# Reordering the work around the first expert tiles of a gated alignment and mixture-of-experts block on one Trainium2 core

## The reference

```python
x = x + jnp.tanh(g_xattn[0]) * align(ctx_1024, layernorm(x))   # dynamic time warping of 154 rows onto 2048, 2 batches
xn = layernorm(x).reshape(4096, 512)
logits = xn @ gate_w.T                                          # 8 experts
w, sel = jax.lax.top_k(logits, 2); w = softmax(w)
expert_out = jnp.einsum('nc,edc->ned', xn, expert_w)
x = x + jnp.tanh(g_ffn[0]) * (w_full of the two chosen experts summed over expert_out)
```

## Time and profile before

| what | value |
| --- | --- |
| median of 3 runs | 602.07 us (599.56 to 602.33) |
| the profiled execution | 599.65 us, of it 597.9 us span |
| PE busy | 457.6 us, 77% |
| DVE busy | 307.6 us, 51% |
| ACT busy | 263.0 us, 44% |
| POOL busy | 225.5 us, 38% |
| granted PE clock, mean | 0.86 of full |

### The profile page before, as it was taken

How to read it: one execution, slowest core, us unless ns; L and a number is a source line. 1 busy time by engine, 2 the same in 40 slices (tenths; PEclk the granted TensorE clock), 3 DMA queues, 4 the chain that set the end, 5 groups by cost and what they waited for, 6 DMA issues and landing times. The chain is left out here.

```text
span 597.9 us, 8208 instructions
## 1 busy us (share of the span) xinstructions
PE 457.6 (77%) x2029; PEld 271.4 (45%) x2029; DVE 307.6 (51%) x1635; ACT 263.0 (44%) x508; POOL 225.5 (38%) x214
## 2 busy tenths in 40 slices
PE   8989655477232304687996989999999999999980
PEld 7989543254122201343443544444454444445440
DVE  7778799999998885898678411101111010111000
ACT  6538778854735402892653223322233332223320
POOL 5550222000000000003428565766657665767522
PEclk9999868668565655796997999999999999999995
DMA  8965334640046001777999686878868787878743
GB/s 289 353 189 190 86 85 117 187 98 2 0 160 263 1 1 36 288 245 231 296 260 309 116 164 122 149 134 144 138 114 153 130 142 136 139 122 152 118 53 35
DMA packets 61386, 88.88 MB, mean 149 GB/s; under 512 B 24933, under 2 KB 25189, under 8 KB 61181
## 3 DMA queue, kind: packets, MB, share of 16 engines
q0 software_dynamic: 16048, 37.31, 35.8%
q1 hardware_dynamic: 38701, 42.64, 21.8%
q10 hardware_dynamic: 6592, 8.42, 4.5%
HBM read 48.92 MB, written 39.43 MB: 148 GB/s over the span
## 5 line engine op out<-in xcount | busy, mean ns | idle before, releaser
L1973 PE MATMUL psum<-big,work 128*128 x560 | 257.1, 602 | 4.3 <-ACT work L1627 4.3
L697 POOL DMA_INDIRECT stage<-x_rows,row_ids x71 | 70.0, 986 | 224.1 <-DVE row_ids L1173 176.0
L1973 PEld LDWEIGHTS psum<-big,work 128*128 128x128 f32 x560 | 102.9, 194 | 108.0 <-issue 108.0
L1323 DVE TENSOR_TENSOR part_scale<-stage,st 128x1 f32<-128x1 f32 x62 | 10.0, 162 | 201.2 <-DMA stage<-x_rows,row_ids 201.2
L717 POOL DMA_INDIRECT out_dram<-prow,row_ids x34 | 61.3, 1802 | 36.0 <-ACT prow L1638 14.2
L717 POOL DMA_INDIRECT out_dram<-tokens,row_ids x36 | 57.2, 1589 | 41.3 <-DMA out_dram<-tokens 15.5
L1638 ACT ACTIVATE tokens<-psum,tile_shares 128x512 f32<-128x512 f32 x36 | 24.7, 687 | 98.4 <-issue 70.5
L1638 ACT ACTIVATE prow<-psum,tile_shares 128x512 f32<-128x512 f32 x34 | 23.3, 687 | 86.8 <-issue 78.6
L1947 PEld LDWEIGHTS psum<-ident,stage 128*128 128x128 f32 x284 | 35.6, 143 | 40.6 <-issue 33.7
L1756 PE MATMUL psum<-ident,stage 128*128 128x128 f32 x128 | 27.7, 401 | 33.3 <-ACT big L1526 20.5
L1627 ACT COPY work<-psum 128x512 f32<-128x512 f32 x71 | 41.0, 578 | 19.2 <-PE psum L1947 14.8
(11 more groups left out here) (388 smaller groups left out, 649.7 us busy)
## 6 DMA issues: line engine op xcount, KB each, us to landing
tokens<-in_x_dram SPq DMA_DIRECT2D x16, 1024.0 KB, 11.8
stage<-in_L_ffn_expert_w_dram ACTq DMA_DIRECT2D x8, 1024.0 KB, 5.6
out_dram<-tokens SPq DMA_DIRECT2D x8, 1024.0 KB, 9.1
x_rows<-tokens SPq DMA_DIRECT2D x7, 1024.0 KB, 7.3
tokens<-dist_rows SPq DMA_DIRECT2D x52, 64.0 KB, 2.1
dist_rows<-work SPq DMA_DIRECT2D x16, 160.0 KB, 2.0
dist_rows<-prow SPq DMA_DIRECT2D x5, 256.0 KB, 10.5
stage<-x_rows,row_ids POOLq DMA_INDIRECT x71
```

Of the source, the lines that this page charges most:

```text
L697: pool.indirect_dma_start(out=xin[:, n % UX, :], out_offset=None, in_=x1_d[0:T, :] if n < FA else x1_d[:, :], in_offset=bass.IndirectOffse ...
L1973: ins = nc.tensor.matmul(psum[:, UP + n % UP, :], xinT[:, n % UX, c, :], expT[:, bass.ds(own, 1), c, :].rearrange("p o d -> p (o d)"), sta ...
```

## The change

Five orders are changed; no matmul is added or removed.

- PE: `invert_first_shares()` stands behind tile 1's expert, not ahead of it. The alignments of tiles 24 to 31 and `rank()` stand behind tile 2, not tile 3.
- ACT: the squares of tiles 16 to 19 stand ahead of the copy of tile 2; three copies out stand ahead of the ten last squares; two one-element activations load the tables of Sqrt and Exp where they stand; the store of the second batch's pairs of shares stands behind `copy_in(5)`.
- DVE: `first_shares()` stands inside `place_choices`, `scales(1)` between the two `lay_lanes`, `pairs_of(1)` ahead of the sets, `ids()` ahead of `own_tiles()`.
- The sets are laid in halves, each member half followed by its number half, and `invert()` waits for the second half in its middle.
- `ids()` keeps its intermediate in `slotf`, not in `owner`, and no longer waits for `s_own`.

```diff
--- before.py
+++ after.py
@@ -442,8 +442,8 @@
         EARLY = 4
         RING = (4, 5, 0, 1, 2, 3)
         AR = len(RING)
-        SQUARED = [[], [16, 17], [18, 19], [20, 21, 22, 23], [24, 25, 26, 27, 28, 29, 30, 31]]
-        ALIGNED = [[], [22, 23], [], [24, 25, 26, 27, 28, 29, 30, 31]]
+        EARLY_SQUARES, MORE_SQUARES, LATE_SQUARES = range(TB, TB + 4), range(TB + 4, TB + 6), range(TB + 6, NT)
+        ALIGNED = [[], [22, 23], [24, 25, 26, 27, 28, 29, 30, 31]]
         LATE = (4, 5, 2, 3, 4, 5, 4, 5, 6, 4, 5, 6, 4, 5, 6, 4)
         BEFORE = [None if t < 4 else [u for u in range(t) if LATE[u] == LATE[t]][-1:] for t in range(TB)]
         FIRST_IDS = 2 * P
@@ -1210,6 +1210,7 @@
                 lnk(v.tensor_tensor_scan(upto, keep[:, :], total, 0.0, ALU.mult, ALU.add))
                 v.tensor_tensor(place, upto, total, ALU.subtract).then_inc(s_gt, 1)
                 ln[0] += 1
+                first_shares()
                 counts = more.rearrange("p (e m) -> p e m", e=E)
                 lnk(v.tensor_tensor(counts, spread(upto[:, KB - 1:KB], [[KB, E], [0, NT]]),
                                     spread(full[:, 0:1], [[0, E], [1, NT]]), ALU.is_gt))
@@ -1267,19 +1268,18 @@
                     v.tensor_tensor(lanes[h][:, :, q * TB:(q + 1) * TB], pattern,
                                     spread(partf[:, 1, (2 * h + q) * TB:(2 * h + q) * TB + 1], [[0, P], [1, TB]]), ALU.is_equal)
 
-            def lay_members():
-
-                for g in (2, 3):
-                    v.wait_ge(s_out[g], 16)
-                    v.wait_ge(s_rows[g], 16 * (GT if g == GB - 1 else 1))
-                v.wait_ge(s_sq, TB)
-                lnk(v.tensor_tensor(sets[:, :, 0, :], spread(partf[:, 0, 0:1], [[1, KB], [0, JB]]),
-                                    spread(tiles[:, 0:1], [[0, KB], [1, JB]]), ALU.is_equal))
-
-            def lay_numbers():
-
-                v.tensor_tensor(sets[:, :, 1, :], sets[:, :, 0, :], spread(numbers[:, 0:1], [[1, KB], [0, JB]]),
-                                ALU.mult).then_inc(s_numl, 1)
+            def lay_sets(h):
+
+                if h == 0:
+                    for g in (2, 3):
+                        v.wait_ge(s_out[g], 16)
+                        v.wait_ge(s_rows[g], 16 * (GT if g == GB - 1 else 1))
+                    v.wait_ge(s_sq, TB)
+                n, i0 = KB // 2, h * KB // 2
+                lnk(v.tensor_tensor(sets[:, i0:i0 + n, 0, :], spread(partf[:, 0, i0:i0 + 1], [[1, n], [0, JB]]),
+                                    spread(tiles[:, 0:1], [[0, n], [1, JB]]), ALU.is_equal))
+                v.tensor_tensor(sets[:, i0:i0 + n, 1, :], sets[:, i0:i0 + n, 0, :],
+                                spread(numbers[:, i0:i0 + 1], [[1, n], [0, JB]]), ALU.mult).then_inc(s_numl, 1)
 
             def pad_places():
 
@@ -1304,8 +1304,7 @@
 
                 v.wait_ge(s_inv, 2)
                 codes_ = psum[:, 7, JB:2 * JB]
-                later = owner
-                v.wait_ge(s_own, 2)
+                later = slotf[:, 0:JB]
                 lnk(v.tensor_scalar(later, codes_, 0.0, float(B * T), ALU.is_lt, ALU.mult))
                 lnk(v.tensor_tensor(later, later, codes_, ALU.add))
                 ins = v.tensor_copy(rows_ids[:, FA:NSEQ], later)
@@ -1353,20 +1352,19 @@
             lay_first_shares()
             for t in (20, 21):
                 add_context(t)
-            first_shares()
             place_choices()
             for t in range(22, NT):
                 add_context(t)
             pad_places()
             lay_lanes(0)
+            scales(1)
             lay_lanes(1)
-            scales(1)
-            lay_members()
             pairs_of(1)
-            lay_numbers()
+            lay_sets(0)
+            lay_sets(1)
             pads()
+            ids()
             own_tiles()
-            ids()
             mark_tiles()
             for n in range(FA, NSEQ):
                 tile_share(n)
@@ -1642,20 +1640,32 @@
                     nc.scalar.mul(yout(n)[:, HC:C], psum[:, 4, HC:C], scale[:, n:n + 1]).then_inc(s_ye, 1)
 
             copy_in(0)
-            for n in range(NSEQ):
-                if n + 1 < NSEQ:
+            copy_in(1)
+            for t in EARLY_SQUARES:
+                squares(t)
+            copy_in(2)
+            nc.scalar.activation(gates[:, 0:1], eps[:, :], ACT.Sqrt)
+            for t in MORE_SQUARES:
+                squares(t)
+            copy_out(0)
+            copy_out(1)
+            copy_in(3)
+            copy_out(2)
+            for t in LATE_SQUARES:
+                squares(t)
+            root(1)
+            copy_in(4)
+            nc.scalar.activation(gates[:, 0:1], eps[:, :], ACT.Exp)
+            shares(1)
+            copy_out(3)
+            copy_in(5)
+            act.wait_ge(s_pair, 2)
+            act.dma_start(x1_d[T:2 * T, C:RW].rearrange("(t p) k -> p t k", p=P),
+                          pairs[:, TB:2 * TB, :]).then_inc(s_sto[1], 16)
+            for n in range(4, NSEQ):
+                if n > 4 and n + 1 < NSEQ:
                     copy_in(n + 1)
-                for t in SQUARED[n] if n < len(SQUARED) else []:
-                    squares(t)
-                if n == len(SQUARED) - 1:
-                    root(1)
                 copy_out(n)
-                if n == len(SQUARED) - 1:
-                    shares(1)
-                if n == len(SQUARED):
-                    act.wait_ge(s_pair, 2)
-                    act.dma_start(x1_d[T:2 * T, C:RW].rearrange("(t p) k -> p t k", p=P),
-                                  pairs[:, TB:2 * TB, :]).then_inc(s_sto[1], 16)
 
         @block.tensor
         def _(pe):
@@ -1916,6 +1926,8 @@
                                  bass.AP(none.tensor, none.offset, [none.ap[0], [0, 3 * JB]]), start=True, stop=False)
                 for i in range(KB):
                     k = i // TB % K
+                    if i == KB // 2:
+                        pe.wait_ge(s_numl, 3)
                     both = sets[:, i, ::-1, :] if k else sets[:, i, :, :]
                     nc.tensor.matmul(psum[:, 7, k * JB:(k + 2) * JB].rearrange("p (s j) -> p s j", s=2),
                                      lanes[i * 2 // KB][:, :, i % (KB // 2)], both, start=False, stop=False)
@@ -1986,11 +1998,12 @@
                     expert(n, own)
                 if n == 0:
                     count()
+                if n == 1:
                     invert_first_shares()
                 if n < len(ALIGNED):
                     for t in ALIGNED[n]:
                         align(t)
-                if n == 3:
+                if n == 2:
                     rank()
                 if n == FA - 3:
                     invert()
```

## The result

The changed kernel takes 592.96 us (median of 4 runs, 592.33 to 594.56). The kernel before, run beside it, took 600.98 (599.56 to 602.33). The ratio is 0.987, with a 95% interval of 0.984 to 0.991. The profiled execution took 592.65 us, with a span of 590.9 against 597.9.

The account below looks back on a forecast made before the run. PE, busy and at full clock from about 340 us, was taken as the bound. T9 6.5 us earlier less 3.1 for a fallen clock gave 3.4 us saved off the 602.07 median: 598.7 us, range 593.5 to 603.0.

Parts of the forecast that it names:

- T9: Start of tile 9's transposes on PE, 334.77 us before; forecast at 328.3, 6.5 us earlier.
- gather 9 to T9: Gather 9's issue at 322.3 to tile 9's transposes: 5.8 us landing under load plus 0.2 for the start.
- stop ahead of tile 9: PE idle of 3.7 us before tile 9, waiting for gather 9.
- clock's cost: PE falls to half clock after the idle before tile 9, costing 3.07 us, taken from tile 6's expert.
- tile 12's stop: PE's wait for a gather before tile 12's transposes, claimed to stay at 1.66 us.
- Steps 1 to 4: Tile 1's expert, alignments, squares and tables moved, sets halved: `invert` starts 316.3, ids come at 322.0, 9.0 us earlier.
- From there on the two kernels run the same chain: From T9 both kernels run alike, so the saving is how far T9 moves, less a fallen clock's cost.
- A: Rival: same landing of gather 9, PE's clock stays; 6.5 us saved, 595.6 us, chance 0.27.
- C: Rival: gather 9 lands as if nothing were in front, at 325.8; 9.0 us saved, 593.1 us, chance 0.13.
- D: Rival: all transfers issued ahead of gather 9 are served first; T9 332.0, 602.4 us, no change, chance 0.17.
- E: Rival, slower: DMA backlog doesn't shrink, T9 stays 334.8, clock loses 3.1 us more; 605.2 us, chance 0.08.
- step 3: ACT's squares behind copies, tables early: tile 6's 4.33 us stop and half clock go; second pairs' store at 308.4.

Follow-up runs that it names:

- repeat: The changed kernel run once more, nothing altered; 594.50 us over 6 runs, ratio 0.990 to the kernel before.
- `before_tokens_held`: The kernel before, with SP holding tokens_out of groups 4 to 7 until gather 9 has landed; 604.78 us, ratio 1.0084 to the kernel before.
- `aligned_late`: The changed kernel with alignments 24 to 31 and the rank behind tile 3 again; 601.07 us, ratio 1.002 to the kernel before.
- `aligned_late_pairs`: The changed kernel with alignments 24 to 31 and rank behind tile 3 again, second pairs' store on SP ahead of tokens_out; 595.71 us, ratio 0.992.
- `squares_old`: The changed kernel with ACT's order of the kernel before; 600.09 us, ratio 0.998 to the kernel before.
- `squares_old_pairs`: The changed kernel with the squares' order of the kernel before and the second pairs' store on SP ahead of tokens_out; 601.35 us, ratio 1.002.

## Why the forecast was half the gain

Up to T9 the mechanism was right, and undoing the order of the squares or of the alignments takes the gain away. Behind T9 it was wrong. Point by point:

| step | forecast | measured |
| --- | --- | --- |
| stop ahead of alignment 24 | 1.5 | 1.25, repeat 1.23 |
| copy of tile 4 starts | 304.0 | 301.32 |
| `invert` starts | 316.3 | 314.07 |
| adds 4 and 5 | end 1.4 after a sets operation | 1.42 and 1.43 after |
| ids | 322.0 | 319.49 |
| gather 9 to T9 | 5.8 + 0.2 | 5.99 (320.93 to 326.92) |
| stop ahead of tile 9 | 3.7 | 4.39, repeat 3.96 |
| clock's cost | 3.07 | 2.74, repeat 1.70 |
| tile 12's stop | still 1.66 | gone, in both executions |

Steps 1 to 4 hold. The times are 2 to 2.7 us earlier than forecast, and 1.57 of that came from further up: DVE starts to mark the last choices at 279.20 before and 277.63 after, and PE's turn of tile 0 already stood 1.52 us earlier (273.01 and 271.49), ahead of the first changed call, ACT's square at 274.19. It is most likely chance: over the 14 profiles of this study, none of which changes DVE's order up to there, the marking starts anywhere between 277.63 and 280.34.

The gather's landing time, taken from a row under load, held (the repeat's is 6.33, and with tokens_out held it is 3.62). T9 moved by 7.85 us; less those 1.57 it is 6.28, for 6.5 forecast. That the two agree is partly luck. The ids came 11.48 us earlier, 9.9 without the chance, for 9.0 forecast; of this, 0.5 is a slip in the prediction's sum (316.3 plus the 5.51 us from `invert` to the ids before, less its 0.3, is 321.5, not 322.0). And gather 9 then left 1.44 us behind the ids, not 0.3, most likely since x1's group 7 landed only at 319.9, a wait that the prediction did not price. The clock's cost is the time from tile 9's to tile 10's transposes, 6.67 us (326.92 to 333.59) less the 3.93 of before (334.77 to 338.70).

**The step that failed** is the sentence "From there on the two kernels run the same chain", with "tile 12's wait still 1.66". They don't. Gather 12 goes out 0.8 us ahead of tile 11's transposes in both kernels: 336.70 for 337.46 in the change, 341.81 for 342.58 before. But in the change it is there within 4.6 us, and before it took 6.46. POOL's timeline before (gather 11, add 8, gather 12), and PE's turn of tile 11:

```profile
336.99 0.99 POOL L697 DMA_INDIRECT stage<-x_rows,row_ids  x1 [0.30 <-issue]
339.92 1.59 POOL L717 DMA_INDIRECT out_dram<-tokens,row_ids  x1 [1.94 <-ACT tokens L1638]
341.81 0.99 POOL L697 DMA_INDIRECT stage<-x_rows,row_ids  x1 [0.30 <-DVE tile_shares L1324]
342.58 0.60 PE L1947 MATMUL psum<-ident,stage 128*128 128x128 f32 x4
```

The windows of the 4 us ahead of it (columns: busy us of PE, PEld, DVE, ACT, POOL, granted clock, DMA share, GB/s), before:

```profile
337.80:341.80 4.00, 4.00 (x14) 1.99 (x13) 0.38 (x2) 1.16 (x2) 1.76 (x2) 1.00 0.54 119
```

And in the change:

```profile
332.70:336.70 4.00, 4.00 (x14) 2.01 (x13) 0.38 (x2) 1.16 (x2) 1.59 (x2) 1.00 0.25 95
```

In the change gather 11 and add 7 were out by 326.96, while PE stood for gather 9; only add 8 is in front of gather 12, and the DMA share is 0.25. Before, add 7, gather 11 and add 8 all went out in the 6.7 us ahead of it, with a share of 0.54.

So the long stop at tile 9 lets the queues run empty and pays back the later one. All 14 profiles fit this. Where PE stood 1.98 us or more ahead of tile 9 (nine of them), gather 11 went out 6.4 us or more ahead of gather 12, and tile 12 was there within 4.6 to 4.9 us, with no stop of more than 0.24 us. In both profiles of the kernel before it was 4.7 to 4.8 us, and the stop came. In the three with tokens_out held, PE stood under 0.7 us ahead of tile 9, and 2.16 to 3.01 ahead of tile 11. But no run tried it alone, so the cause stays a reading.

The price is 348.27 less the 342.58 + 3.87 at which tile 12 would have followed tile 11: 1.82 us. The sum then closes: 7.85 - 2.74 + 1.82 = 6.93, for a span shorter by 7.0. Without those 1.57 us it is 5.4. The repeat gives 7.25 - 1.70 + 1.34, less 0.07 of slack between tiles 11 and 12, = 6.8, of it 0.61 upstream. So the change is worth some 5.4 to 6.2 us by its own traces, not 3.4: 1.8 and 1.3 us for a stop that was left in the sum, 0.3 and 1.4 for a clock that costs less than at tile 6. The medians gave 8.0 here and 5.9 in the repeat; that the rest is chance in the first half and in the medians is not shown.

**The rivals.** A (the clock stays) fell: 5.92 and 4.94 for the expert behind the stop. C fell: the gather took 6.0 us, not 3.5 (with tokens_out held it took 3.6). D fell: q0 had 41.5% in 311 to 324, beside q1.

E, the slower one, did not come about here but is real, by a mechanism that the prediction passed over. Gather 9 waits for three things besides its place on POOL. The prediction followed the ids and the backlog in front of the gather itself. Of ACT's store of the pairs, another of these three, it said only that it "joins the DMA load". With it behind tokens_out the gather goes out at 331.90, T9 is 335.38 and the time is 602.18: rival E's landing after 331.7, from one small transfer. In the change that store is 0.77 us on the safe side of it. The prediction's own step 3 had it at 308.4 and tokens_out at about 309, which is on the same side by 0.6 us; nothing was said about what lay on the other. That the change came out on the right side was luck, as far as the prediction goes.

## What to carry to other kernels

List everything that the gated instruction waits for and when each lands, the small transfers too: a small store of many tiny packets that was issued behind a large one of as many landed only about when that did, 19.5 us later, so issue it ahead of the bulk. A stop that is removed or made longer can change the stops after it; the tail is "the same chain" only if the next gathers meet the same queues. Holding back bulk traffic that must go out anyway moves a stop, and saves nothing unless there is slack for it.

## What the runs showed of the hardware

**Tiny packets.** The changed kernel's DMA in 305 to 310, when both stores of pairs are under way (packets, rate, queues, then issues with their time to landing):

```profile
DMA packets 4199, 0.27 MB, mean 54 GB/s; under 512 B 4083, under 2 KB 4083, under 8 KB 4199
...
q1 hardware_dynamic: 2080, 0.05, 25.9%
q10 hardware_dynamic: 2003, 0.02, 22.9%
...
x_rows<-tokens SPq DMA_DIRECT2D x1, 1024.0 KB, 14.4
...
x_rows<-st ACTq DMA_DIRECT2D x1, 16.0 KB, 8.9
```

The engines are 0.81 busy and move 54 GB/s. Each small store has 2048 packets, and nearly all of ACT's go in these 5 us. x1's group 7, issued behind SP's pairs at 305.50, takes 14.4 us for 1 MB. That fits gather 9's start at 320.93, 1.4 us behind the ids, though the trace names no releaser for it.

**The adds under DVE.** Four adds in two kernels ended 1.42 or 1.43 us after the end of a two-input DVE operation, at lengths of 2.2 and 4.3 us, and behind three of them the next such operation followed without a gap. So an add is held until the running operation ends, and gets in between two. The engines of this kernel therefore meet at more than semaphores.

**The clock after a stop.** The length of the stop alone does not decide it. The clearest pair differs up to there only in what SP holds back: behind 4.33 us the expert of tile 6 took 6.67 us in the kernel before and 5.39 in `before_tokens_held`. So the 3.07 us that the prediction took from the first was itself one draw. An expert behind a stop of 2.41 us took 5.39 us in `aligned_late` and 3.69 in `aligned_late_pairs`, at the same place. Behind 4.93 us it took 5.39 in `squares_old` and 5.08 in `squares_old_pairs`, behind 4.39 it took 5.92, behind 2.39 (`squares_old_pairs`, tile 9) 3.60. Behind only 1.98 it took 5.29, at a granted clock of 0.68 (`squares_old`, tile 9):

```profile
337.47 0.66 PE L1948 MATMUL psum<-ident,stage 128*128 128x128 f32 x4 [1.98 <-DMA stage<-x_rows,row_ids]
337.96 5.29 PE L1974 MATMUL psum<-big,work 128*128 x8
```

The estimate from the nearest stop was right in sign, and off by up to 1.4 us in size.
